# A merged attention kernel: idle mask products on TensorE at three stage starts, loads and setup work in another order, and a row sum shared with GpSimd

## The chip, the cores and the metric

The kernel runs on one core of a Trainium2 chip. The metric is the time of one execution on the device in microseconds (us), as the median of several runs. The core has TensorE (PE in the profile, with PEld for its weight loads), VectorE (DVE), ScalarE (ACT), GpSimd (POOL) and SyncE (SP), which here only issues transfers.

## The reference

Two layers are computed one after the other over 32 sequences of 112 tokens with 512 features.

```
# layer 0: gated attention to a memory of 375 rows of 256 features
mp    = memory @ W_mem
attn  = softmax(x @ mp.T / sqrt(512));  mc = attn @ mp
x     = rmsnorm(x + sigmoid([x, mc] @ W_gate.T + b) * mc) * norm_w
# layer 1: every token has one of two experts (v or l)
q,k,v = rmsnorm(x) @ (v_qkv or l_qkv), rotary on q and k
x     = x + causal_attention(q, k, v) @ (v_dense or l_dense)      # 16 heads of 32
x     = x + cross_attention(rmsnorm(x) @ cq_w, ctx @ ckv_w) @ cdense_w
x     = x + glu_mlp(rmsnorm(x), expert v or l)
```

Products are in float32 and most are split in three: high times high, high times low, low times high. ACT makes a high part, and DVE or POOL subtracts it from the source to get the low part.

## The kernel before

There are six stages, A to F, one after the other on every engine. Each engine runs its own list, in the order in which the code writes it; semaphores carry the dependencies.

**Stage A** (about 0 to 357 us in the profile) is layer 0, in 8 groups of 4 sequences. PE's list for a group is `gate(g-1)`, `attended` (probabilities times memory), `turn(g-1)`, `context(g)`, `u(g+1)` and `s0(g+1)` (scores). At the start (`g == 0`) it also has `setup_pe_wc` (a product of two weights) and `setup_pe` (small products which give each token its slot by expert). `setup_dve_slots` is a chain of some 40 tiny DVE operations that ends in a memset. DVE's list at the start is: softmax of group 0, low parts of the product of weights, `attended`, low parts of memory 1 and x 1, the setup chain, `u_low(1)`, `softmax(1)`. ACT's list begins group 0 with six chunks of weights (`ring_high`), and only then `setup_act_wc`. PE's `transposed(0, ...)` stands behind a wait for `mem_n`.

**Ring.** Weights of all stages pass through a ring of 8 chunks of 128x512: SP loads one, ACT makes its high part (L199), POOL its low part (L177), PE uses it. SP issues all transfers in one list.

**Stage B** (366 to 647) makes q, k and v for 8 tiles of up to 512 tokens; tile 0 has 256. For each tile ACT squares, DVE adds an epsilon (L929), POOL takes the power (`power`, L826), DVE scales (`norm`, L934), PE transposes (`turn`, L897). POOL has the low parts of 8 chunks ahead of `power(0)`.

**Stage C** (649 to 900) is the causal attention, one sequence a step. PE writes a mask product (L1099: a 112x112 identity by a 112x448 mask, bf16) and adds the scores (L1104); DVE takes the row maximum (L1161) and subtracts it (L1166); ACT takes the exponential (L1069); PE transposes, ACT copies out (L1063), PE multiplies by v, ACT copies (`raw`, L1066); DVE sums the 1792 probabilities of a row into 16 heads (L1172), takes the reciprocal and scales (L1181); POOL scatters the result. PE's list for step s is `scores(s)`, transposes and context of s-1, `turn_in(s + 2)` (L1088), `turn_out(s - 1)`. In 14 of the steps (3 to 8 and 10 to 17) ACT also casts 512 columns of weights. SP's list is: q and k rows of sequences 0 and 1, v of 0 to 2, then `e_weights`, `q_weights` and 8 ring chunks for stage D, and only then the q and k rows of sequence 2.

**Stages D, E, F** are the dense layer with the cross queries (907 to 1062), the cross attention one sequence a step (1064 to 1662), and the mlp. D begins with `turn_context(0)` (L1295), which waits for rows that the last scatter of C has written. E's list on PE has two steps more than sequences, in which it drains.

## Time and profile before

| | |
|---|---|
| median of 3 runs | 2385.78 us (2385.53 to 2386.26) |
| the profiled execution | 2383.2 us, span 2381.4 us |
| granted TensorE clock, mean | 0.97 |
| PE / DVE / ACT / POOL busy | 2174.7 / 1342.4 / 1073.9 / 841.8 us |
| busy share of PE | 91% |

The span is what the instructions cover; some 2 us lie around it. A granted clock of 1.00 is 2.4 GHz, one of 0.50 is 1.2 GHz. A busy share close to 100% on PE says only that products follow each other there.

### The profile page before, as it was taken

What the parts mean: (1) busy time and instruction counts of PE and PEld (TensorE: products, weight loads), DVE (VectorE), ACT (ScalarE), POOL (GpSimd) and SP (SyncE); (2) the same over time, 40 slices, a digit from 0 to 9 for tenths busy, and PEclk for the clock granted to TensorE, in tenths of its full rate; (3) what the DMA queues carried; (4) which work ended last, traced back from release to release, by engine and by line L of the source; (5) the groups of instructions that cost most, each with busy time, mean ns of one, the idle gap of its engine ahead of it and who ended that gap; (6) DMA issues with size and microseconds to landing.
All of it is one profiled execution on the core that took longest, in us unless ns stands there. A gap on an engine that the chain in (4) does not pass through costs nothing.

```text
span 2381.4 us, 46501 instructions
## 1 busy us (share of the span) xinstructions
PE 2174.7 (91%) x19368; PEld 1820.1 (76%) x19368; DVE 1342.4 (56%) x1887; ACT 1073.9 (45%) x1842; POOL 841.8 (35%) x706
## 2 busy tenths in 40 slices
PE   5899996999879988988999999997899999999998
PEld 4899985887756667876777777775788888888887
DVE  4655545877669994435666666663444434435332
ACT  4334434333157774533555555554434434334432
POOL 1101017677513213540222111110555555555553
PEclk8999998999979998997999999999899999999999
DMA  6334335565454445632111111110643443443331
GB/s 201 133 115 141 123 88 180 202 234 208 146 169 130 138 121 215 253 149 74 49 41 41 49 39 49 41 33 29 222 146 124 137 131 120 148 133 109 111 116 45
DMA packets 107057, 293.56 MB, mean 123 GB/s; under 512 B 14424, under 2 KB 18360, under 8 KB 100216
## 3 DMA queue, kind: packets, MB, share of 16 engines
q1 hardware_dynamic: 86624, 229.63, 29.9%
q0 software_dynamic: 18720, 60.29, 6.9%
q8 instruction: 154, 2.52, 0.4%
q10 hardware_dynamic: 1504, 0.68, 0.1%
q14 instruction: 55, 0.45, 0.1%
HBM read 221.36 MB, written 69.18 MB: 122 GB/s over the span
## 4 chain that ended last, share of the span: by engine, by line
PE 73%; DVE 17%; ACT 4%; DMA 3%; issue 2%; POOL 1%; SPq 0%; POOLq 0%; DVEq 0%; ACTq 0%
PE ps L109 19%; PE ps L111 18%; PE ps L110 18%; PE ps L1554 4%; PE ps L1573 3%; PE ps L1591 3%; DVE f_arena L1166 3%; DVE c_max L1161 3%; DVE f_arena L962 3%; ACT f_arena L1474 3%; DVE c_sum L1172 2%; DMA f_arena<-mem_t 1%; PE ps L607 1%; DVE f_arena L958 1%; PE ps L1576 1%
## 5 line engine op out<-in xcount | busy, mean ns | idle before, releaser
L109 PE MATMUL ps<-r_arena 128*128 128x512 f32 (+6 forms) x2410 | 905.6, 376 | 39.1 <-DVE r_arena L177 18.2
L177 POOL TENSOR_TENSOR r_arena<-f_arena,r_arena 128x512 fp32r<-128x512 f32 (+1 forms) x438 | 586.5, 1364 | 868.7 <-ACT r_arena L1455 438.4
L111 PE MATMUL ps<-r_arena 128*128 128x512 f32 (+6 forms) x2410 | 883.8, 367 | 0.0
L110 PE MATMUL ps<-r_arena 128*128 128x512 f32 (+6 forms) x2410 | 883.6, 367 | 0.0
L109 PEld LDWEIGHTS ps<-r_arena 128*128 128x128 f32 (+2 forms) x2410 | 456.0, 189 | 131.8 <-issue 37.6
L111 PEld LDWEIGHTS ps<-r_arena 128*128 128x128 f32 (+2 forms) x2410 | 455.9, 189 | 66.1
L110 PEld LDWEIGHTS ps<-r_arena 128*128 128x128 f32 (+2 forms) x2410 | 457.0, 190 | 60.1
L199 ACT CAST r_arena<-f_arena 128x512 fp32r<-128x512 f32 x400 | 235.5, 620 | 171.3 <-PE ps L111 131.7
L1675 DVE TENSOR_REDUCE e_negmax<-ps 112x3 f32<-112x1125 f32 (+1 forms) x160 | 225.2, 1408 | 106.7 <-PE ps L1554 103.8
L1474 ACT ACTIVATE f_arena<-ps 125x1792 f32<-125x1792 f32 x96 | 159.9, 1666 | 97.9 <-PE ps L1576 97.4
L1959 DVE SCALAR_TENSOR_TENSOR f_arena<-f_arena,ps 128x512 f32<-128x512 f32 (+1 forms) x88 | 57.4, 652 | 234.8 <-ACT f_arena L1850 234.8
L1854 ACT CAST r_arena<-f_arena 128x512 fp32r<-128x512 f32 (+1 forms) x88 | 52.2, 593 | 248.7 <-DVE f_arena L1963 248.7
L177 DVE TENSOR_TENSOR r_arena<-f_arena,r_arena 128x512 fp32r<-128x512 f32 (+4 forms) x141 | 111.1, 806 | 73.3 <-ACT r_arena L1854 58.0
L1573 PE MATMUL ps<-r_arena 32*125 32x224 f32 x2304 | 100.9, 285 | 39.8 <-ACT f_arena L1474 39.4
L1573 PEld LDWEIGHTS ps<-r_arena 32*125 32x125 f32 x2304 | 82.1, 185 | 66.3 <-ACT f_arena L1474 50.5
L1554 PE MATMUL ps<-r_arena 32*112 32x376 f32 x1536 | 121.4, 355 | 9.5 <-DVE e_negmax L1675 4.9
L1963 DVE SCALAR_TENSOR_TENSOR f_arena<-f_arena,ps 128x512 f32<-128x512 f32 (+1 forms) x88 | 57.6, 654 | 104.5 <-PE ps L111 104.1
L1850 ACT ACTIVATE f_arena<-ps 128x512 f32<-128x512 f32 (+1 forms) x88 | 50.2, 570 | 138.4 <-PE ps L111 138.4
L177 DVE TENSOR_TENSOR r_arena<-ps,r_arena 128x224 fp32r<-128x224 f32 (+3 forms) x130 | 75.0, 591 | 64.7 <-ACT r_arena L1257 25.1
L1034 POOL DMA_INDIRECT ctx_rows<-f_arena,slot_all x32 | 30.0, 936 | 200.2 <-DVE f_arena L1181 200.2
L1554 PEld LDWEIGHTS ps<-r_arena 32*112 32x112 f32 x1536 | 73.3, 172 | 32.9 <-DVE e_negmax L1675 14.5
L452 POOL TENSOR_TENSOR a_rstd<-a_ss,minus_half 112x2 f32<-112x2 f32 x16 | 11.3, 707 | 233.7 <-DVE a_ss L719 233.7
(197 smaller groups left out, 2714.9 us busy)
## 6 DMA issues: line engine op xcount, KB each, us to landing
f_arena<-weights SPq DMA_DIRECT2D x400, 256.0 KB, 3.0
f_arena<-rows SPq DMA_DIRECT2D x14, 1160.0 KB, 5.2
f_arena<-qk_rows SPq DMA_DIRECT2D x32, 448.0 KB, 3.9
f_arena<-mem_e SPq DMA_DIRECT2D x32, 376.0 KB, 3.1
f_arena<-mem_t SPq DMA_DIRECT2D x16, 750.0 KB, 9.8
f_arena<-mem_n SPq DMA_DIRECT2D x8, 1500.0 KB
h_rows<-f_arena SPq DMA_DIRECT2D x7, 1160.0 KB, 4.8
f_arena<-h_rows SPq DMA_DIRECT2D x7, 1160.0 KB, 5.2
```

What stands on the lines that cost most here:

```text
L109: first = pe.matmul(out, w_hi, x_hi, start=start, stop=False)
L110: pe.matmul(out, w_hi, x_lo, start=False, stop=False)
L111: return first, pe.matmul(out, w_lo, x_hi, start=False, stop=stop)
L177: return engine.tensor_tensor(out, source, high.bitcast(F32), ALU.subtract)
L199: act.copy(w_hi[:, m % RING, :], w_raw[:, m % RING, :]).then_inc(w_hi_made, 1)
L962: dve.tensor_tensor(b_qk[:, j, which * DIM:(which + 1) * DIM].rearrange("p (h d) -> p h d", h=HEADS), by_cos, by_sin, ALU.add).then_inc(b_ ...
L1161: dve.tensor_reduce(c_max[:].rearrange("p (m j) -> p m j", j=4), now, AX_X, ALU.max).then_inc(*d_steps.up())
L1166: dve.tensor_tensor(c_prob[b % 2].rearrange("p (m j) s -> p m j s", j=4), now, c_max[:].rearrange("p (m j) -> p m j", j=4).unsqueeze(3).to ...
L1474: act.activation(e_pt[:, u], ps[0:KC, 4:8, 0:4 * SEQ], ACT.Exp).then_inc(e_exp, 1)
L1554: last = pe.matmul(ps[0:SEQ, h - s_heads[u][0], 0:CEVEN], q[r, h // 4, :], k[r, h // 8, :], start=n == 0, stop=n == 2)
L1573: pe.matmul(ps[0:KC, 4 + i, out], k[r, t, m], q[r, 2 * t:2 * t + 2, :], start=n == 0, stop=False)
L1675: dve.tensor_reduce(e_negmax[:, b % 2, heads[0]:heads[-1] + 1], ps[0:SEQ, 0:len(heads), 0:CTX], AX_X, ALU.max, negate=True).then_inc(e_max ...
```

## The change

It adds idle mask products on PE (their result is never read) ahead of stages B, C and D: 64, 12 and 28 of them. It also reorders SP's, ACT's, PE's and DVE's lists at the start of A; puts POOL's `power(0)` between the fourth and the fifth low part in B; moves the loads of `e_weights`, `q_weights` and D's chunks behind those of the q and k rows of sequences 2 and 3 in C; lets POOL fold half of the heads (adds the two halves of 56 columns) so that DVE sums 896 and 448 elements in place of 1792; and writes E's last two steps out in another order.

```diff
+        def keep_busy(pe, bank, count):
+            for _ in range(count):
+                pe.matmul(ps[0:SEQ, bank, 0:NT], ident_b[0:SEQ, 0:SEQ], causal[:].rearrange("p m s -> p (m s)"),
+                          start=True, stop=True)
@@ stage A, SP @@
-            for c in range(CT, A_CHUNKS):
+            for c in range(C_MC, C_GATE):
                 ring_load(sp, c, weights[c])
+            load_memory_t(1, 0)
             load_x(1)
+            for c in range(C_GATE, A_CHUNKS):
+                ring_load(sp, c, weights[c])
+            load_memory_t(1, 1)
@@ stage A, ACT @@
                 if g == 0:
-                    for m in range(CT, RING):
+                    setup_act_wc(act)
+                    for m in range(C_MC, C_GATE):
                         ring_high(act, m)
-                    setup_act_wc(act)
-                    setup_act_consts(act)
...
                 if g == 0:
-                    memory_high(1, 1)
+                    memory_high(1, 0)
+                    setup_act_consts(act)
+                    for m in range(C_GATE, RING):
+                        ring_high(act, m)
@@ behind the four mc copies @@
+                if g == 0:
+                    memory_high(1, 1)
@@ stage A, PE @@
-                    pe.wait_ge(a_mn_loaded, 16 * (g + 1))
                     if g == 0:
                         transposed(g, 0)
                         transposed(g, 1)
+                    pe.wait_ge(a_mn_loaded, 16 * (g + 1))
...
-                if g == 0:
-                    setup_pe(pe)
                 if g + 1 < GROUPS:
                     u(g + 1)
                     s0(g + 1)
+                if g == 0:
+                    setup_pe(pe)
@@ stage A, DVE @@
-                    memory_low(1, 1)
+                    memory_low(1, 0)
                     x_low(1)
-                    setup_dve(dve)
-                    setup_dve_total(dve)
-                    setup_dve_ranks(dve)
-                    setup_dve_slots(dve)
+                    memory_low(1, 1)
                 if g + 1 < GROUPS:
                     u_low(g + 1)
+                    if g == 0:
+                        setup_dve(dve)
+                        setup_dve_total(dve)
+                        setup_dve_ranks(dve)
+                        setup_dve_slots(dve)
                     softmax(g + 1)
@@ stage B, POOL and PE @@
-            for c in range(RING):
+            for c in range(RING // 2):
                 ring_low(pool, b_chunk(0, c))
             power(0)
+            for c in range(RING // 2, RING):
+                ring_low(pool, b_chunk(0, c))
             power(1)
...
+            keep_busy(pe, 2, 64)
             turn(0)
@@ stage C, SP @@
-            sp.dma_start(e_w_raw, e_weights).then_inc(e_w_loaded, 16)
-            sp.dma_start(q_w_raw, q_weights).then_inc(e_w_loaded, 16)
-            for n in range(CT):
-                base = sp.value_load(base_d[0:1, n:n + 1], min_val=W_D, max_val=W_D + D_CHUNKS)
-                for c in range(D_CHUNKS):
-                    ring_load(sp, M_D + D_CHUNKS * n + c, chunk_at(base, c))
             for b in range(2, BATCHES):
                 sp.wait_ge(c_tk, b - 1)
                 load_qk(b)
                 if b >= 3:
+                    if b == 3:
+                        ... (the same two loads and 8 ring loads)
                     sp.wait_ge(c_ctx, b - 2)
                     load_v(b)
@@ stage C, POOL, DVE, PE @@
+            def fold(b):
+                pool.wait_ge(c_exp, b + 1)
+                if b == 0:
+                    pool.wait_ge(b_v_scattered, 16 * BLOCKS)
+                if b:
+                    pool.wait_ge(c_summed, 2 * b)
+                half = c_prob[b % 2][:, HEADS // 2:HEADS, :]
+                pool.tensor_tensor(c_fold, half[:, :, 0:SEQ // 2], half[:, :, SEQ // 2:SEQ], ALU.add).then_inc(c_folded.sem, 1)
...
-                dve.tensor_reduce(c_sum[:], c_prob[b % 2], AX_X, ALU.add).then_inc(c_summed, 1)
-                dve.wait_ge(c_summed, b + 1)
+                dve.tensor_reduce(c_sum[:, 0:HEADS // 2], c_prob[b % 2][:, 0:HEADS // 2, :], AX_X, ALU.add).then_inc(c_summed, 1)
+                dve.wait_ge(*c_folded.at(b + 1))
+                dve.tensor_reduce(c_sum[:, HEADS // 2:HEADS], c_fold, AX_X, ALU.add).then_inc(c_summed, 1)
+                dve.wait_ge(c_summed, 2 * (b + 1))
...
             pe.wait_ge(b_v, BLOCKS)
+            keep_busy(pe, 7, 12)
             turn_in(0)
@@ stage D, PE @@
+            keep_busy(pe, 0, 28)
             turn_context(0)
@@ stage E, PE, behind the loop over s < BATCHES @@
+            b = BATCHES - 1
+            maximum_turn(b)
+            scores_by_key(b, 0)
+            context(b - 1, 1)
+            turn(b - 1)
+            scores_by_key(b, 1)
+            back(b - 1)
+            scores_by_key(b, 2)
...
```

Under `if b == 3:` stand the two loads and the 8 ring loads that were taken out above. In E, PE's list goes on with `dense(30)`, both parts of `context(31)`, `turn(31)`, `back(31)` and `dense(31)`. In E, ACT's order at step 32 becomes: exponential 0, `raw`, exponential 1, copy of the turned context, `e_out` (L1507), exponential 2. Before, PE had `context(30, 1)`, `turn(30)` and `back(30)` ahead of `scores_by_key(31, 0)`.

## Rows read from the trace of the kernel before

**Rows 1.** Windows view, start of stage C: length, busy, granted clock, DMA share, GB/s

```profile
655.00:677.00 22.00, 8.22 (x58) 5.99 (x56) 4.05 (x2) 4.53 (x7) 0.00 (x0) 0.50 0.77 253
```

**Rows 2.** Timeline, stage A: start us, us, engine line op, idle before and releaser

```profile
36.95 1.57 PE L597 MATMUL ps<-ident,f_arena 112*125 112x112 f32 x6 [7.75 <-issue]
43.62 2.90 PE L607 MATMUL ps<-f_arena 125*128 125x112 f32 x12 [5.11 <-DVE f_arena L709]
58.29 0.41 PE L288 MATMUL ps<-f_arena 112*32 112x128 f32 x2 [0.28 <-DVE f_arena L315]
71.20 0.17 DVE L385 TENSOR_SCALAR f_arena<-f_arena 128x2 int32<-128x2 f32 x1
72.04 0.62 PE L109 MATMUL ps<-r_arena 128*112 128x376 f32 x1 [4.67 <-DVE r_arena L666]
76.41 1.05 DVE L673 TENSOR_REDUCE a_max<-ps 112x1 f32<-112x375 f32 x2 [3.98 <-PE ps L111]
77.75 0.36 PE L109 MATMUL ps<-r_arena 128*128 128x448 f32 x1
81.59 0.64 ACT L504 ACTIVATE f_arena<-ps,half_b 128x448 f32<-128x448 f32 x1 [1.12 <-PE ps L111]
```

**Rows 3.** Timeline, start of stage B

```profile
363.58 9.80 POOL L177 TENSOR_TENSOR r_arena<-f_arena,r_arena 128x512 fp32r<-128x512 f32 x8
370.99 2.42 DVE L929 TENSOR_SCALAR t_ss<-t_ss 128x2 f32<-128x2 f32 x1 [10.45 <-ACT f_arena L858]
374.23 0.88 DVE L934 TENSOR_SCALAR f_arena<-f_arena,t_rstd 128x512 f32<-128x512 f32 x2 [0.83 <-POOL t_rstd L826]
375.17 1.97 PE L897 MATMUL ps<-ident,f_arena 128*128 128x128 f32 x8 [18.23 <-DVE f_arena L934]
401.09 4.76 DVE L934 TENSOR_SCALAR f_arena<-f_arena,t_rstd 128x512 f32<-128x512 f32 x4 [0.90 <-POOL t_rstd L826]
```

**Rows 4.** Timeline, start of stage C

```profile
653.62 1.73 PE L1088 MATMUL ps<-ident,f_arena 112*128 112x112 f32 x8 [6.47 <-DMA f_arena<-qk_rows]
657.58 1.70 PE L1099 MATMUL ps<-causal,ident_b 112*112 112x448 bf16 x4
659.55 5.37 SPq L186 DMA_DIRECT2D f_arena<-weights  x8
664.97 0.91 SPq L1006 DMA_DIRECT2D f_arena<-qk_rows  x2
674.12 1.76 PE L1088 MATMUL ps<-ident,f_arena 112*128 112x112 f32 x8 [13.06 <-DMA f_arena<-qk_rows]
679.22 2.02 DVE L1161 TENSOR_REDUCE c_max<-ps 112x16 f32<-112x1792 f32 x1 [14.01 <-PE ps L1104]
```

**Rows 5.** Groups of DVE in 677 to 900: count, busy us, mean ns, idle before

```profile
L1172 DVE TENSOR_REDUCE c_sum<-f_arena 112x16 f32<-112x1792 f32 x32 | 64.3, 2008 | 0.0
```

**Rows 6.** Timeline, steady steps of stage C

```profile
683.06 0.53 ACT L1066 COPY f_arena<-ps 128x448 f32<-128x448 f32 x1 [0.52 <-PE ps L1126]
684.18 0.92 PE L1099 MATMUL ps<-causal,ident_b 112*112 112x448 bf16 x4
686.16 2.02 DVE L1161 TENSOR_REDUCE c_max<-ps 112x16 f32<-112x1792 f32 x1
689.78 0.53 ACT L1066 COPY f_arena<-ps 128x448 f32<-128x448 f32 x1 [0.52 <-PE ps L1126]
745.69 1.70 ACT L1069 ACTIVATE f_arena<-f_arena 112x1792 f32<-112x1792 f32 x1
752.63 1.70 ACT L1069 ACTIVATE f_arena<-f_arena 112x1792 f32<-112x1792 f32 x1
```

**Rows 7.** Timeline, start of stage D

```profile
906.83 1.97 PE L1295 MATMUL ps<-ident,f_arena 128*128 128x128 f32 x8 [7.62 <-DMA f_arena<-ctx_rows]
```

**Rows 8.** Chain that ended last, start of stage D

```profile
912.97 1.75 PE ps L1295 x16
```

**Rows 9.** Timeline, end of stage E

```profile
1655.71 1.36 PE L1591 MATMUL ps<-f_arena 125*32 125x112 f32 x48 [0.48 <-ACT f_arena L1474]
```

More of the change, by code:

```diff
@@ L414, in a_sp, with load_memory_t @@
         def a_sp(sp):
-            def load_memory_t(g):
-                for t in range(CT):
-                    sp.wait_ge(a_m_lo, CT * g + t)
-                    sp.dma_start(memt, mem_t[g][:, t, :]).then_inc(a_mt_loaded, 16)
+            def load_memory_t(g, t):
+                sp.wait_ge(a_m_lo, CT * g + t)
+                sp.dma_start(memt, mem_t[g][:, t, :]).then_inc(a_mt_loaded, 16)
             def load_x(g):
@@ L434, in a_sp @@
             load_memory_n(0)
-            for c in range(CT, A_CHUNKS):
+            for c in range(C_MC, C_GATE):
                 ring_load(sp, c, weights[c])
+            load_memory_t(1, 0)
             load_x(1)
+            for c in range(C_GATE, A_CHUNKS):
+                ring_load(sp, c, weights[c])
+            load_memory_t(1, 1)
             for g in range(1, GROUPS):
-                load_memory_t(g)
                 if g >= 2:
+                    for t in range(CT):
+                        load_memory_t(g, t)
                     sp.wait_ge(a_fused, KT * (g - 1))
@@ L505, in a_act @@
                                        bias=half_b[:, t:t + 1], scale=0.5).then_inc(a_tanh, 1)
-                    if t in ((0, 3) if g else (0,)) and g + 1 < GROUPS:
+                    if g and t in (0, 3) and g + 1 < GROUPS:
                         memory_high(g + 1, t // 3)
@@ L754, in a_dve @@
                     attended(0, 1)
-                    memory_low(1, 0)
                 if g < GROUPS:
@@ L991, in build_xattn @@
             "c_pt", "c_pt_made", "c_ctx", "c_raw", "c_turned", "c_out", "c_summed"))
+        c_folded = Later(a_powered, 2 * GROUPS)
         c_scattered = [sem(f"c_scattered{i}") for i in range(2)]
@@ L1027, in c_sp @@
                 if b >= 3:
+                    if b == 3:
+                        sp.dma_start(e_w_raw, e_weights).then_inc(e_w_loaded, 16)
+                        sp.dma_start(q_w_raw, q_weights).then_inc(e_w_loaded, 16)
+                        for n in range(CT):
+                            base = sp.value_load(base_d[0:1, n:n + 1], min_val=W_D, max_val=W_D + D_CHUNKS)
+                            for c in range(D_CHUNKS):
+                                ring_load(sp, M_D + D_CHUNKS * n + c, chunk_at(base, c))
                     sp.wait_ge(c_ctx, b - 2)
@@ L1507, in e_act @@
                     act.copy(e_out[b % 2], ps[0:SEQ, 3, :]).then_inc(e_cd_out, 1)
+                if 1 <= s < BATCHES:
+                    exponents(s - 1, 1)
                 if 1 <= s <= BATCHES:
-                    for u in range(1, KEY_UNITS):
-                        exponents(s - 1, u)
+                    exponents(s - 1, 2)
         def e_pe(pe):
@@ L1627, in e_pe @@
             scores(0, 0)
-            for s in range(BATCHES + 2):
+            for s in range(BATCHES):
                 if s < 2:
@@ L1633, in e_pe @@
                     keys(s + 1)
-                if 1 <= s <= BATCHES:
+                if s:
                     maximum_turn(s - 1)
-                if s < BATCHES:
-                    scores(s, 1)
+                scores(s, 1)
                 if s >= 2:
@@ L1647, in e_pe @@
                     back(s - 2)
-                if s < BATCHES:
-                    scores(s, 2)
-                if 1 <= s <= BATCHES:
+                scores(s, 2)
+                if s:
                     scores_by_key(s - 1, 0)
@@ L1653, in e_pe @@
                     dense(s - 2, 0)
-                if s < BATCHES:
-                    scores(s, 3)
+                scores(s, 3)
                 if s >= 2:
                     dense(s - 2, 1)
-                if 1 <= s <= BATCHES:
+                if s:
                     scores_by_key(s - 1, 1)
-                if s < BATCHES:
-                    scores(s, 4)
-                if 1 <= s <= BATCHES:
+                scores(s, 4)
+                if s:
                     scores_by_key(s - 1, 2)
@@ L1665, in e_pe @@
                     scores(s + 1, 0)
-                if 1 <= s <= BATCHES:
+                if s:
                     context(s - 1, 0)
+            b = BATCHES - 1
[6 more added lines that the diff above has]
+            scores_by_key(b, 2)
+            for k in range(CT):
+                dense(b - 1, k)
+            for t in range(CT):
+                context(b, t)
+            turn(b)
+            back(b)
+            for k in range(CT):
+                dense(b, k)
         def e_dve(dve):
```

13 lines of the change are left out of this document (10 added, 3 removed).

## The prediction, as it was put on record

> **What bounds the kernel now.** The page first. PE is busy for 91% of the span and the mean granted clock is 0.97, so in A, B, D, E and F the sum of the products is nearly the time; idle mask products cannot shorten these. What can be had lies where PE stands still or runs at 1.2 GHz, and in C, where it is not the bound. So I read the windows view at the borders of the stages and found four holes, then the timeline of each.
>
> (a) Start of C. In 22 us PE is busy for 8.2 and the clock is 0.50 [rows 1]. The timeline says why: SP issues the q and k rows of sequence 2 at 665.0, behind 8 ring chunks and two larger loads, and PE gets them at 674.1 [rows 4]. PE's list has `turn_in(2)` ahead of `scores(1)`, so DVE waits 14.0 us for its second maximum [rows 4].
>
> (b) Steps of C. DVE's maximum comes back after 6.94 us [rows 4, 6]; DVE has no idle time in them, and one of its four larger operations is the row sum of 2.01 us [rows 5]. But two other loops are close behind. ACT's exponential comes back after 6.94 us in a step with a cast [rows 6], with nothing idle between. And in the step from 683.06 to 689.78, which has no cast and in which ACT's copy (L1066) sets PE's start, that copy comes back after 6.72 us: turn out, masks, scores, transposes, four copies, context, copy [rows 6]. The reader is to see three loops: DVE 6.94, ACT and PE 6.72, ACT with a cast 6.94.
>
> (c) Start of A: PE has the memory rows at 36.95 but starts `attended` only at 43.62, because DVE stands in its list behind the low parts of the weight product [rows 2]. Later `s0(1)` waits 4.7 us for `u_low(1)`, which stands behind the setup chain on DVE [rows 2].
>
> (d) Starts of B and D: PE idles 18.2 and 7.6 us for data and starts at half clock [rows 3, 7].
>
> **The sum, part by part.**
>
> *Stage C, order of the loads.* The bytes between v and the q/k rows of sequence 2 are 1 MB, 0.5 MB and 8 times 0.25 MB. Without them those rows are issued some 7 us earlier, at about 658, with only 0.7 MB of v ahead. I take 661.5 for their landing. DVE's first maximum and subtraction end at 665.2 (679.22 less the 14.01 idle) [rows 4]; `scores(1)` cannot begin before that. At half clock masks and scores take some 3.6 us (four masks are 1.70) [rows 4], so the second maximum would be at 668.8 and the gain 10.4. What is queued behind the moved loads: v of 3 and q/k of 4 wait for SP to issue the ten loads (about 6 us), and are needed two steps later; ACT waits for `e_weights` at step 2, over 10 us after their issue. I cost both at nothing; if cover failed, each would cost its lateness once, under 3 us.
>
> *Stage C, 12 masks.* They follow 2.4 us after the last product of B (PE's idle time began at 647.15 [rows 4]) and end before the first rows come at 653.62, at either pace: at full clock 12 are at most 2.8 (four in 0.92, so at most 0.23 each), at half at most 5.1 (four in 1.70, so at most 0.43) [rows 4, 6]; the latter would end at 654.4, 0.8 late. If the clock stays at 2.4 GHz, both `turn_in`, masks and scores of two steps are faster: 2.2 us by the first maximum, 1.5 by the second, together up to 3.7. But PE has gaps of one to two us there that could bring the clock down again. I take 2.1 of 3.7. Start of C together: 12.5, between 9 and 14.
>
> *Stage C, the fold.* 1792 elements take 2.01 us [rows 5]. A maximum over 375 takes 0.53 (two in 1.05 [rows 2]), so an element costs 1.48 / 1417 = 1.04 ns; by this line, an estimate, 896 and 448 take 1.07 and 0.61, and the two overlap a little: 0.37 less a step. POOL's fold of 448 is about 1.1 us (a low part of 512 is 1.22 [rows 3]), can begin with the sum of the step before and is due a whole step later; hidden. But the loop of ACT and PE allows 0.21 only (6.94 less 6.72), in the 17 steps without a cast; in the 14 with one nothing. 17 x 0.21 = 3.6. Bounds: 0, and 31 x 0.37 = 11.5.
>
> *Stage B.* `power(0)` stands behind eight low parts, to 373.4; DVE's epsilon, ready at 371.0, takes 2.42 us for two columns [rows 3]: it is held up until POOL is through. With four low parts ahead, POOL is free at 368.5, the power is made at 371.9 and `norm(0)` can begin 2.3 us earlier. But now four low parts run beside it. Where that is so, `norm` took 4.76 us for four operations [rows 3], 1.19 each, against 0.44 each alone. So two take 2.4 in place of 0.88, and 1.5 of the 2.3 are lost. If they wait for all four low parts (to 376.8), they end at 377.7, 2.6 late. The 64 masks start at 356.9; at full clock they take at most 14.7 and end by 371.6, ahead of `turn(0)`; at half clock at most 27.5, and they could hold PE up. They follow dense products without a gap, so I take the former and 0.1 for a faster `turn(0)`. Sum 0.9, between -2.5 and 2.5.
>
> The Trainium skill, "SBUF — State Buffer", section Who interferes with whom, says that a `tensor_scalar` may take the port pair that VectorE and GpSimd share, as an exclusive lock for a whole instruction, while a reduction never does. The long epsilon agrees with it. By the rule the fold disturbs none of DVE's sums in C, as I assume, and `norm(0)` is held up as I cost it. It speaks against the new place of `power(0)`: if POOL keeps the pair from one low part to the next, the case with 377.7 is the one.
>
> *Stage A.* `attended` starts at 36.95 in place of 43.62, now that DVE's lows of the weight product come before the chunks (PE then waits for memory alone). From 43.62 to 58.29 is `attended` and `context`, 14.7 with some waits; then `u(1)` of 24 products at 0.205, the wait for its lows (1.5) and `s0(1)`, 5.7 (72.04 to 77.75, cold) or 4.2 warm [rows 2]. New: 36.95 + 14.7 + 4.9 + 1.5 + 4.2 = 62.3, against 77.75. But `softmax(1)` stands behind the setup chain, and this chain now needs `setup_pe`, which is behind `s0(1)`. From `setup_pe` to the chain's end were 13.1 us (58.29 to 71.37), of which about one is done earlier now: `softmax(1)` at 74.4 against 76.41. ACT has its exponentials ahead of the `tanh` that PE's third tile of `gate(0)` waits for: 4.1 us later (81.59 less 1.12 less 76.41) they are done, tanh 0.64, so PE goes on at 79.1. Before, the third tile began at 85.4 (77.75 and two tiles of 3.8) [rows 2]. Gain 6.3, less 1.5 because PE idles some 7 us and restarts at half clock (`s0(1)` above shows the price: 5.7 for 4.2), less 1.5 for DVE's `x_low(1)` and `memory_low` beside POOL's low parts. 3.3, between 0 and 6.
>
> *Stage D, 28 masks.* They start when C's last turn ends (899.2, 906.83 less 7.62 [rows 7]), at half clock after C's thin tail. If the clock rises after some 4 us of them (10 masks), as it did behind other starts, they take 8 us: about 907, with the rows at 906.83. At 2.4 GHz the 8 transposes and the 12 products behind them, which now take 6.1 us (to 912.97 [rows 8]), take some 4. Gain 1.9; all masks at half clock (12.0) would make it -4.3, which I take as the lower end.
>
> *Stage E.* The last exponential moves behind `e_out(30)`, which waits for `dense(30)`. Walking the new order with the rows' durations puts it at 1655.9 against 1655.7 [rows 9]. Nothing, within 1 either way.
>
> Sum: 12.5 + 3.6 + 0.9 + 3.3 + 1.9 + 0 = 22.2. The profiled execution of 2383.2 (its span and 1.8 around it) becomes 2361.0; it lies 2.6 under the median, so the median becomes 2363.6.
>
> **Rivals.**
> 1. *The fold pays in full.* DVE has no idle time, which speaks for it; the 6.72 of ACT and PE and the 6.94 with a cast speak against. Gain 11.5 for 3.6: 2355.7. 0.12.
> 2. *POOL keeps the port, and A's head start is spent on waits.* By the lock of the epsilon row, `norm(0)` ends 2.6 late (-3.5 against mine), and A gives 0 (-3.3): 2370.4. 0.15.
> 3. *The moved loads only move the wait.* If the rows of sequence 2 were late for another reason, such as v's scatter at the end of B, the start of C would give 4 in place of 12.5: 2372. The 3.5 MB ahead of them speak against it. 0.06.
> 4. *Slower: the fold holds DVE up.* If each fold stopped a DVE operation for its length of 1.1 us, 31 steps would grow by 1.1 less 0.2: 28 us against the other 18.6, so 2395. It decides from 0.6 us a step. POOL's stream holds the epsilon of B up, which speaks for it; that POOL runs low parts in 14 of C's steps and the mean sum is 2.01 all the same [rows 5] speaks against. 0.03.
>
> My forecast has 0.64.
>
> **From cases to numbers.** 2363.6, range 2354 to 2372: rivals 1 and 2 lie in it, 3 at its edge, 4 outside. 0.2% is 4.8 us, about what a measurement of this kernel can tell from no change. Faster by more 0.95, within 0.02, slower 0.03.
>
> **What would show it.** Second maximum of C near 666 in that profile less the shifts of A and B, with no wait for q/k rows; steps of 6.7 and 6.9, with DVE idle behind the scores; L1172 as two groups near 1.07 and 0.61; `norm(0)` near 1.2 us each; the third tile of `gate(0)` after about 7 us of idle PE; masks in B ending before the norm; stage D's first second at full clock. Wrong would be: masks that end after their data, a wait of DVE for the fold, or a new wait of C's steps 2 to 4 for rows or v.

## The result, and the profile after

The changed kernel takes 2372.64 us (median of 4 runs, 2371.06 to 2374.28) against 2386.02 (4 runs) of the kernel before beside it: a ratio of 0.9943, 95% interval 0.9926 to 0.9960. The gain is 13.4 us where 22.2 were forecast, and the time lies 0.6 us above the range. Its profiled execution is the longest of the four: 2374.28 us, span 2372.4, mean granted clock 0.975.

Three more series of the unchanged kernel, each beside the kernel before, gave 0.9920 (0.9904 to 0.9937), 0.9928 (0.9914 to 0.9941) and 0.9929 (0.9910 to 0.9949). The mean of the four ratios is 0.9930, some 16.7 us. The forecast was 0.9907. So the sign held, and the largest term, the load order, held too. A quarter of the forecast gain is missing by the mean of the four series, and 40% of it by the first.

First the windows view, columns as in [rows 1] (length; busy us of PE, PEld, DVE, ACT and POOL; granted clock; DMA share; GB/s). The first line answers to [rows 1]. It is the same stretch after the last copies of v, which come 1.8 us sooner now: PE is busy for 15.3 us of 22 and not 8.2, and the clock is 0.77 and not 0.50. The next three lines of the changed kernel are places where PE ran at half clock and where nothing had been forecast. The last line is of the kernel before, at the end of E: full clock throughout.

```profile
653.20:675.20 22.00, 15.25 (x187) 11.35 (x188) 10.74 (x9) 9.04 (x14) 2.12 (x2) 0.77 0.88 283
376.00:392.00 16.00, 13.46 (x59) 11.28 (x58) 10.66 (x21) 8.48 (x19) 8.64 (x7) 0.86 0.29 86
1044.00:1052.00 8.00, 6.62 (x43) 6.62 (x44) 1.33 (x3) 0.89 (x2) 1.61 (x2) 0.79 0.28 108
1638.00:1656.00 18.00, 12.01 (x146) 8.80 (x146) 1.47 (x4) 4.43 (x7) 1.87 (x2) 0.72 0.15 47
...
1643.00:1662.00 19.00, 12.78 (x265) 9.44 (x265) 2.77 (x7) 7.24 (x8) 0.93 (x1) 1.00 0.15 45
```

Then the timeline, start of A (answers to [rows 2]), of B ([rows 3]) and of C ([rows 4]). The lines are of the changed kernel, apart from the one at 384.15, which is `turn(1)` of B in the kernel before.

```profile
37.25 2.90 PE L620 MATMUL ps<-f_arena 125*128 125x112 f32 x12 [5.16 <-DMA f_arena<-mem_n]
80.53 0.74 PE L109 MATMUL ps<-r_arena 128*128 128x448 f32 x1 [7.79 <-ACT f_arena L512]
...
353.07 12.27 PE L216 MATMUL ps<-causal,ident_b 112*112 112x448 bf16 x64
368.83 5.30 POOL L177 TENSOR_TENSOR r_arena<-f_arena,r_arena 128x512 fp32r<-128x512 f32 x4
368.87 2.89 DVE L951 TENSOR_SCALAR f_arena<-f_arena,t_rstd 128x512 f32<-128x512 f32 x2 [0.83 <-POOL t_rstd L840]
371.82 1.97 PE L913 MATMUL ps<-ident,f_arena 128*128 128x128 f32 x8 [6.48 <-DVE f_arena L951]
380.80 3.50 PE L913 MATMUL ps<-ident,f_arena 128*128 128x128 f32 x16 [2.54 <-DVE f_arena L951]
...
384.15 1.97 PE L897 MATMUL ps<-ident,f_arena 128*128 128x128 f32 x16 [3.15 <-DVE f_arena L934]
...
647.48 2.48 PE L216 MATMUL ps<-causal,ident_b 112*112 112x448 bf16 x12 [2.14 <-ACT f_arena L901]
651.72 0.99 PE L1119 MATMUL ps<-ident,f_arena 112*128 112x112 f32 x8 [1.75 <-DMA f_arena<-qk_rows]
653.50 1.66 PE L1119 MATMUL ps<-ident,f_arena 112*128 112x112 f32 x8 [0.80 <-DMA f_arena<-qk_rows]
654.91 1.59 SPq L1028 DMA_DIRECT2D f_arena<-v_rows  x3
656.54 0.89 SPq L1025 DMA_DIRECT2D f_arena<-qk_rows  x2
657.92 2.02 DVE L1193 TENSOR_REDUCE c_max<-ps 112x16 f32<-112x1792 f32 x1 [13.85 <-PE ps L1135]
663.95 1.75 PE L1119 MATMUL ps<-ident,f_arena 112*128 112x112 f32 x8 [6.11 <-DMA f_arena<-qk_rows]
665.50 1.70 PE L1130 MATMUL ps<-causal,ident_b 112*112 112x448 bf16 x4
668.32 2.02 DVE L1193 TENSOR_REDUCE c_max<-ps 112x16 f32<-112x1792 f32 x1 [6.32 <-PE ps L1135]
```

The reader is to see: `attended` starts 6.4 us sooner, but PE stands 7.8 us ahead of the third tile of `gate(0)`; the epsilon takes 0.17 and not 2.42 (its row starts at 367.88), but `norm(0)` takes 2.89 beside POOL's low parts; the 64 masks end at 365.3, and 6.5 us later `turn(0)` runs at half clock as before; `turn(1)` takes 3.5 us for 16 transposes, where the kernel before had 1.97, behind a wait of 3.15 us. At C the second maximum is at 668.3 (679.2 in [rows 4]), and PE still waits 6.1 us for the rows of sequence 2, though they are issued 8.4 us sooner.

DVE's groups in stage C ([rows 5]) and two exponentials in a step with a cast and two in one without ([rows 6]):

```profile
L1204 DVE TENSOR_REDUCE c_sum<-f_arena 112x8 f32<-112x896 f32 x32 | 34.4, 1075 | 0.0
L1206 DVE TENSOR_REDUCE c_sum<-f_arena 112x8 f32<-112x448 f32 x32 | 19.5, 609 | 0.0
```

```profile
741.24 1.70 ACT L1100 ACTIVATE f_arena<-f_arena 112x1792 f32<-112x1792 f32 x1
748.18 1.70 ACT L1100 ACTIVATE f_arena<-f_arena 112x1792 f32<-112x1792 f32 x1
...
870.54 1.70 ACT L1100 ACTIVATE f_arena<-f_arena 112x1792 f32<-112x1792 f32 x1
872.32 1.14 POOL L1064 TENSOR_TENSOR f_arena<-f_arena 112x448 f32<-112x448 f32 x1 [4.17 <-ACT f_arena L1100]
877.21 1.70 ACT L1100 ACTIVATE f_arena<-f_arena 112x1792 f32<-112x1792 f32 x1
```

6.94 with a cast and 6.67 without; the sums take 1.08 and 0.61, as the line through the two rows had it, and DVE never waits for the fold (L1064).

Start of D ([rows 7]; the last line is of the chain of work, [rows 8]) and end of E ([rows 9]):

```profile
885.86 7.10 PE L216 MATMUL ps<-causal,ident_b 112*112 112x448 bf16 x28
893.78 1.10 PE L1329 MATMUL ps<-ident,f_arena 128*128 128x128 f32 x8 [0.82 <-DMA f_arena<-ctx_rows]
...
898.18 1.75 PE ps L1329 x16
```

```profile
1641.67 0.63 PE L111 MATMUL ps<-r_arena 128*112 128x512 f32 x1
1643.02 4.38 PE L1631 MATMUL ps<-f_arena 125*32 125x112 f32 x96 [0.72 <-issue]
1650.78 0.77 PE L109 MATMUL ps<-r_arena 128*112 128x512 f32 x1 [0.86 <-DVE r_arena L177]
1653.72 0.59 ACT L1546 COPY f_arena<-ps 112x512 f32<-112x512 f32 x1 [3.42 <-PE ps L111]
```

The masks end 0.8 us before D's rows come, and the first turn is at full clock. So it was in two more of the four profiles. In the third the masks ran at full clock all along, took 5.5 us, ended 2.3 us before the rows, and the turn ran at half clock (1.96). In E's tail, in the execution shown, most of the last two `dense` and the 96 products of the last context run at half clock: 0.63 for 512 columns, where the kernel before had 0.40, and 4.38 for 96, where it had 1.36 for 48.

**Stage by stage.** One execution is moved by a microsecond or two by the places where the clock falls. So the table takes the time between two marks in several profiles: two of the kernel before, four of the changed one. A mark is the start of a row of the timeline; a merged row, such as the four last copies of v, has the start of its first instruction.

```
us                                   before          changed (4)                   gain   forecast
start to turn(0) of B            375.17 374.91   371.82 371.55 371.55 371.56       3.4     4.2
turn(0) to last copy of v        272.01 272.02   273.56 273.67 273.94 272.22      -1.3     0
copy of v to second maximum       32.04  32.67    22.94  22.28  22.97  21.18      10.0    12.5
second to last maximum of C      207.83 207.82   204.78 204.79 204.79 204.72       3.1     3.6
last maximum to last output       12.26  12.66    13.06  12.67  12.12  13.08      -0.3     0
to the last turn_normed of D     156.72 156.30   155.02 155.24 155.98 155.05       1.2     1.9
to the first maximum_turn of E    47.02  49.10    49.00  47.01  49.06  48.97      -0.5     0
E's tail (last maximum_turn to
  last copy to e_out)             19.18  20.08    22.91  22.90  22.27  22.91      -3.1     0
from there to the end            719.25 716.35   718.68 718.69 718.73 718.91      -1.0     0
```

The gains are differences of the means. They add up to 16.1 at the end of D's products and to 11.5 over all rows. One stretch isn't in the table, the body of E: 539.9 and 539.4 before, and 540.6, 543.6, 544.8 and 537.1 after. With its 1.9 us the profiled executions differ by 9.6 us in the mean. Two of the four bodies are 4.8 us longer for a reason that is not of this change (last section), which is 2.4 in the mean; so the timed gain, not the 9.6, measures the change.

Forecast row 1 is A's 3.3 and B's 0.9; all of B's forecast gain lay there. Its 3.4 is on the high side. In eleven other profiles with the same code in A, with the masks and without, `turn(0)` of B came at 371.6 to 373.6.

### The profile page after: what moved, and what is told of

The parts are those of the page before. It is cut to its first block, busy times and chain, and to the rows that moved or that the text cites. A ratio compares the mean times of both kernels' runs of the same rounds, so it can differ in the third digit from the quotient of the medians.

```text
span 2372.4 us, 46806 instructions
## 1 busy us (share of the span) xinstructions
PE 2201.2 (93%) x19472; PEld 1838.7 (78%) x19472; DVE 1335.8 (56%) x1919; ACT 1072.9 (45%) x1842; POOL 880.1 (37%) x738
## 4 chain that ended last, share of the span: by engine, by line
PE 78%; DVE 9%; ACT 7%; DMA 3%; issue 2%; POOL 1%; SPq 0%; POOLq 0%; DVEq 0%; ACTq 0%
PE ps L109 19%; PE ps L111 18%; PE ps L110 18%; PE ps L1594 4%; PE ps L1631 4%; PE ps L1613 3%; DVE f_arena L979 3%; ACT f_arena L1509 2%; PE ps L1146 2%; ACT f_arena L1094 1%; DMA f_arena<-mem_n 1%; PE ps L620 1%; DVE f_arena L975 1%; PE ps L1157 1%; DVE f_arena L971 1%
## 5 line engine op out<-in xcount | busy, mean ns | idle before, releaser
L1594 PEld LDWEIGHTS ps<-r_arena 32*112 32x112 f32 x1536 | 73.6, 173 | 32.8 <-DVE e_negmax L1727 14.4
L979 DVE TENSOR_TENSOR f_arena<-f_arena 128x512 f32<-128x512 f32 x60 | 91.4, 1524 | 2.1
```

Of the source, the lines that this page charges most:

```text
L979: dve.tensor_tensor(b_qk[:, j, which * DIM:(which + 1) * DIM].rearrange("p (h d) -> p h d", h=HEADS), by_cos, by_sin, ALU.add).then_inc(b_ ...
L1594: last = pe.matmul(ps[0:SEQ, h - s_heads[u][0], 0:CEVEN], q[r, h // 4, :], k[r, h // 8, :], start=n == 0, stop=n == 2)
```

## The experiments

They came in four groups, each timed beside runs of the kernel before, whose medians in the groups were 2393.84, 2383.57, 2393.79 and 2385.34 us. Times are to be compared inside a group, or by ratio; the intervals reach some 3 to 5 us to either side, so the marks carry the argument.

**1. The changed kernel again** (three times, no edit).

> The changed kernel once more, nothing edited. Two theories of why 15 us gained by the start of D were only 9.0 at the end of the profiled run. (1) The losses belong to the code: this run's profile then has the same half-clock stretches (1046 to 1049, 1640 to 1647, turn(1) of B at 381) within 1 us, and a span of 2372. (2) They are chance, a matter of the moment at which a gap of PE falls: some of these stretches are gone or stand elsewhere, and the span differs by 1 to 4 us, with the difference in D and E. The timed median stays near 2372.6 in both cases.

> The changed kernel a third time, as the measure for the three kernels beside it, and for what repeats from one execution to the next. What repeats belongs to the change: turn(1) of B at half clock (3.5 us for 16), second maximum of C 22 to 23 us behind the last copy of v, steps of C of 6.7, the tail of E (from the last maximum_turn to the last e_out copy) 22.9 us against 19.2 and 20.1 in two profiles of the kernel before. What does not repeat is chance: the end of D and the start of E, 47.0 or 49.0 us.

> The changed kernel as the measure for the three beside it: from turn(0) of B to the last copy of v 273.6 to 273.9 us, turn(1) of 16 transposes 3.5 us, the tail of E 22.3 to 22.9 us.

Medians 2375.80, 2377.68 and 2367.04 us. The second profile against the first, the stretch in which D's last queries run:

```profile
1044.00:1052.00 8.00, 6.01 (x48) 5.81 (x48) 0.35 (x1) 2.14 (x4) 2.62 (x3) 1.00 0.24 94
376.00:392.00 16.00, 13.54 (x59) 11.39 (x58) 10.91 (x21) 8.42 (x18) 8.80 (x7) 0.86 0.26 80
```

Here the clock didn't fall at 1046 (0.79 in the first profile, 1.00 in this one, in the same code), but it did again at 381. Both theories hold, each for other places. What repeats is `turn(1)` of B (granted clock 0.85 or 0.86 in 376 to 392, four of four) and E's tail. D's end with E's start takes 47 or 49 us by chance, in the kernel before as well.

**2. The kernel before again.**

> The kernel before once more, nothing edited, for a second profile. If the difference that opens behind 908 us is chance (when the clock falls in a gap of PE, and how long ACT takes to start in E), this profile shows other half-clock stretches in D and E than the first, and a span that differs by 1 to 7 us; the stage marks up to the last maximum of C stay within 1 us of the first (second maximum 679, last one 887). If it is the code, both profiles of the kernel before agree within 0.5 us throughout.

Span 2381.3, the first 2381.4; but 49.1 in place of 47.0 at the start of E, and 2.9 us less from E's last output to the end. Up to the end of C both agree within 1 us.

**3. Loads held back until the q/k rows have landed.**

```diff
                     if b == 3:
+                        sp.wait_ge(c_qk_loaded[0], 32)
+                        sp.wait_ge(c_qk_loaded[1], 32)
                         sp.dma_start(e_w_raw, e_weights).then_inc(e_w_loaded, 16)
```

> The changed kernel, but SP waits until the q and k rows of sequences 2 and 3 have landed before it issues e_weights, q_weights and the 8 chunks. Theory: the rows of sequence 2 took 7.4 us from issue to landing because these loads shared the DMA engines with them; alone they land in some 3.5 us, PE's second turn_in group starts at about 660 instead of 664, the second maximum comes at about 664.5 instead of 668.3, and the kernel gains 3.5 us (2369). Rival: the rows are slow for another reason (the v rows ahead of them, their own size); then they land after 7 us as before and nothing is gained (within 0.5 us). A second rival: the loads are now late for ACT's first cast, a wait there of some 2 us, which would eat half of the gain.

```profile
657.60 0.90 SPq L1025 DMA_DIRECT2D f_arena<-qk_rows  x2
663.19 1.76 PE L1121 MATMUL ps<-ident,f_arena 112*128 112x112 f32 x8 [3.67 <-DMA f_arena<-qk_rows]
```

With nothing behind them the rows take 5.6 us, not 3.5. In the first three profiles of the changed kernel PE had them at 664.0, 662.5 and 663.9, 7.4 us after issue in the first; in the fourth, with all ten loads behind them as ever, at 660.4, 4.2 us after issue (656.14). So what follows the rows doesn't decide alone. What goes ahead may, which these rows suggest and don't show: the q/k rows of sequence 4 are issued here just behind the 8 chunks, and PE had them at 679.53, 7.8 us from issue. With that wait and a stretch at half clock behind it the steps of C took 3.2 us more (207.95). 2378.66 us against 2375.80: the theory falls.

```profile
671.75 0.43 SPq L1025 DMA_DIRECT2D f_arena<-qk_rows  x1
679.53 0.98 PE L1121 MATMUL ps<-ident,f_arena 112*128 112x112 f32 x8 [1.50 <-DMA f_arena<-qk_rows]
```

**4. The q/k rows of sequence 2 ahead of v.**

```diff
+            sp.wait_ge(c_tk, 1)
+            load_qk(2)
             sp.wait_ge(b_v_scattered, 16 * BLOCKS)
             for b in range(3):
                 load_v(b)
-            for b in range(2, BATCHES):
+            for b in range(3, BATCHES):
```

> The changed kernel, but SP issues the q and k rows of sequence 2 as soon as turn_in(0) has freed their buffer, ahead of the wait for v's scatter and the three v loads. New theory of why these rows came at 664: with e_weights, q_weights and the chunks held back they still landed 5.6 us after issue, so most of the lateness lies in their issue at 656.5, behind v's scatter (654.8) and 0.7 MB of v. Here they are issued at about 653 and land by 658; scores(1) then waits for DVE's subtraction (about 662) and not for rows, the second maximum comes at 665.5 instead of 668, and 2 to 3 us are gained. Rival: v of sequence 0 now comes so late that context(0) waits, and nothing is gained.

```profile
659.14 1.48 PE L1121 MATMUL ps<-ident,f_arena 112*128 112x112 f32 x8
663.51 1.63 PE L1132 MATMUL ps<-causal,ident_b 112*112 112x448 bf16 x4 [2.89 <-DVE f_arena L1200]
666.98 2.02 DVE L1195 TENSOR_REDUCE c_max<-ps 112x16 f32<-112x1792 f32 x1 [3.62 <-PE ps L1137]
```

PE no longer waits for rows but for DVE's subtraction (L1200): the wait that the forecast had named as the floor. The second maximum comes 7.7 us after the first (10.4, 8.3, 10.5 and 7.1 in the changed kernel) and 21.6 after the copy of v, 0.7 less than the changed kernel's mean. Ratio 0.9940 (0.9923 to 0.9956), in another group: no gain that the time can show. The lateness is where the new theory has it, and the edit takes the wait away; what it was worth is 0.7 in the mean, not 2 to 3, as the fourth profile of the changed kernel had its rows early by itself.

**5. Without masks, masks alone, without the fold.**

> The changed kernel without the 64, 12 and 28 mask products. By my sum the masks gave 0.1 in B, 2.1 at the start of C and 1.9 at the start of D, so it would be 4 us slower. By what the changed kernel's trace shows it is less: in B turn(0) ran at half clock with the masks as well, and turn(1) took 3.5 us with them and 2.0 in the kernel before; without masks turn(1) is at full clock again and B gains 1.5. At C both turn_in groups take 1.7 again (1.0 and 1.7 with masks), at D the eight transposes 2.0 (1.1 with masks). Together 1 to 2.5 us slower. Rival: the clock's later course changes with them so that nothing is left of it, within 0.5 us.

> The kernel before with the 64, 12 and 28 masks alone. The run without masks says that they do little: the start of C took 22.7 us without them and 22.3 to 23.2 with them, and the eight transposes that open B ran at half clock either way. So: B and C unchanged within 0.5 us, D 1.1 us less if the eight transposes of its first turn and the products behind them run at 2.4 GHz, the whole 0.5 to 1.5 us faster than before, which its time cannot show and its stage marks can. Rival: with PE's rows of sequence 0 two us later than in the changed kernel the masks end too early and the clock is half again at C (4 masks 1.70).

> The changed kernel without the fold: DVE sums all 1792 elements again, POOL does nothing in their place. Theory (three loops): steps of 6.94 us again, from the second maximum to the last 3.1 to 3.6 us longer, the time 3.3 us more. Rival (the fold pays in full, 0.37 in each of 31 steps): 11.5 us more. Rival (the fold holds DVE up through the shared port): the changed kernel's steps would be as long, and this one is not slower.

Without masks: ratio 0.9945 (0.9928 to 0.9962). C's start takes 22.7 us (22.3 in the mean with them), D up to its last turn 156.15 (155.3 with them), B 273.7. So the load order is worth 9.6 us (32.36 in the mean of the kernel before, less 22.73). For the 12 masks 0.4 is left, less than the four profiles with them differ among themselves (21.2 to 23.0), and for the 28 masks 0.8. It reaches `turn(0)` 1.6 us later, but that was lost in A, ahead of the first mask. Its `turn(1)` fell to half clock too:

```profile
373.26 1.97 PE L913 MATMUL ps<-ident,f_arena 128*128 128x128 f32 x8 [18.52 <-DVE f_arena L950]
382.24 2.98 PE L913 MATMUL ps<-ident,f_arena 128*128 128x128 f32 x16 [3.63 <-DVE f_arena L950]
```

The masks of B thus neither warmed `turn(0)` (1.97 with and without) nor are they what cools `turn(1)`. Masks alone on the kernel before: 2391.77 us against 2393.79, ratio 0.9991 (0.9981 to 1.0001). C's start 32.8, as without them; D 155.1. By this ratio some 2 of 17 us, and at the most 4.5, come from the idle products that the title names first. The run without masks would leave them 3.6 (0.9945 against the mean of 0.9930), inside the intervals.

Without the fold the steps from the second to the last maximum took 208.0 us, 3.2 more than the 204.8 with it, and the sums are back in one group:

```profile
L1202 DVE TENSOR_REDUCE c_sum<-f_arena 112x16 f32<-112x1792 f32 x32 | 64.3, 2008 | 0.0
```

So the fold gives what the three loops allow. Neither rival holds: not 11.5 us, and no loss.

**6. POOL's old order at the start of B.**

```diff
-            for c in range(RING // 2):
+            for c in range(RING):
                 ring_low(pool, b_chunk(0, c))
             power(0)
-            for c in range(RING // 2, RING):
-                ring_low(pool, b_chunk(0, c))
```

> The changed kernel with POOL's eight low parts ahead of power(0) again; the masks and everything else stay. Theory (port): the earlier power gains little, because norm(0) then takes 2.9 us beside POOL's low parts and not 0.9; here power(0) comes some 2 us later, norm(0) takes 0.9, turn(0) starts within 0.5 us of 371.8, and the time is within 0.7 us of the changed kernel's. Rival: the earlier power is worth its whole 2.3 us; then this kernel is 2 us slower. Beside that the second turn may fall at half or at full clock, which would show as 1.5 us either way at 381.

`norm(0)` takes 0.88 there and `turn(0)` starts at 372.00 (371.82). But equal code had `turn(0)` anywhere from 371.6 to 373.6. From the last transposes of A to `turn(0)` it is 20.7 us here, and 20.5 to 21.0 in the four profiles of the changed kernel. So the earlier power is worth 0.2 us or nothing, not 0.8. The median, 2376.21 against 2375.80, says the same.

**7. Twelve masks ahead of `turn(1)`.**

```diff
+                    if c == 2 and n == 0:
+                        keep_busy(pe, 2, 12)
                     if c == 2 and n + 1 < TILES:
                         turn(n + 1)
```

> The changed kernel with 12 idle mask products ahead of turn(1) of stage B, where PE waits 2.5 us. If the clock falls in this wait, they keep it at 2.4 GHz: turn(1) takes 2.0 in place of 3.5, the step from turn(1) to turn(2) 21.8 in place of 23.4, and B is 1.5 us shorter. Rival: the fall was set in motion earlier, by the idle 6.5 us ahead of turn(0) and the thin products behind it; then turn(1) stays at half clock, and the masks give nothing.

```profile
379.65 2.43 PE L216 MATMUL ps<-causal,ident_b 112*112 112x448 bf16 x12
382.15 1.97 PE L913 MATMUL ps<-ident,f_arena 128*128 128x128 f32 x16
```

`turn(1)` takes 1.97 again, from it to the next turn 21.78 (23.3 to 23.4 in the changed kernel, 21.8 before). The 1.5 us are the clock, and PE's wait of 2.5 us just ahead is the place where masks pay. The time, 2369.45 against 2367.04, can't show 1.5 us.

**8. E's tail.** The old order twice, and the new one with 24 masks in its waits (`keep_busy(pe, 0, n)` with n 2, 4, 6, 3, 3, 3 and 3 ahead of the steps for which PE waits).

> The changed kernel with the end of stage E in the order of the kernel before, on PE and ACT. In the profiled run the last e_out copy had 12.2 us of gain before the tail and 8.4 behind it. (1) If the new order costs time by itself, this kernel is some 2 to 3.7 us faster (about 2369.5). (2) If it was only that the clock fell at 1640 in the new order, in about every run, the same gain, and the profile shows the old order at full clock until the last dense. (3) If both orders are equal and the clock falls in either now and then, the change is within 1 us.

> The changed kernel with the old order of E's tail, a second time. If the new order costs 3 us by itself, the tail takes 19.2 to 20.1 here, as in the kernel before, and the time is 3 us less than the changed kernel's. If the clock decides whatever the order, the tail takes 22.3 again, with a half-clock stretch in it, and the time is the same within 1 us.

> The changed kernel with idle mask products in the gaps of E's new tail (24 in all, two to six in each wait of PE). If the tail is long because the clock falls in it (PE stands still for about 1 us four times, and its dense(30) and the 96 products of the last context then run at half clock), the masks hold the clock, and the tail takes 19 to 20 us in place of 22.9: 3 us gained. If the order itself is the longer one, or the clock falls all the same, nothing is gained or some tenths lost.

The old order took 22.3 and 19.2 us, the new one with masks 19.4. The timeline, first the old order's second profile, then the new order with masks:

```profile
1641.59 1.36 PE L1626 MATMUL ps<-f_arena 125*32 125x112 f32 x48 [0.48 <-ACT f_arena L1509]
1646.33 0.49 PE L109 MATMUL ps<-r_arena 128*112 128x512 f32 x1 [0.86 <-DVE r_arena L177]
```

```profile
1646.58 1.36 PE L1631 MATMUL ps<-f_arena 125*32 125x112 f32 x48 [0.16 <-ACT f_arena L1509]
1651.31 0.49 PE L109 MATMUL ps<-r_arena 128*112 128x512 f32 x1 [0.29 <-DVE r_arena L177]
```

At full clock the two orders are equal, as forecast (`best3`, below, has 19.2 with the new one). The new one took 22.05 to 22.91 in all eleven profiles that had it without masks, with part of it at half clock; the old one 19.2, 19.2, 20.1, 22.3 and 22.3 in five. Both 22.3 are of the groups in which the body of E was 4.8 us longer (last section). In the other groups the old order had 19.2 to 20.1 three times of three, and the new one 22.9 six times of six. So the order and the execution decide together whether the clock falls. `e_tail_masks` has the ratio 0.9917 against 0.9928 beside it (2372.33 and 2377.68 us); the old order 2375.03 against 2375.80 and 2368.82 against 2367.04, no difference that can be told.

**9. More holes filled, and all together.** `filled_gaps` is the changed kernel with edit 4, 96 masks in place of 64, and 12, 20 and 48 masks ahead of D's last queries, E's first keys and F's first turn. `best3` adds edit 7 and the masks of 8.

> A further kernel: the changed one with the q and k rows of sequence 2 issued ahead of v, 96 masks in place of 64 ahead of B (so that they end at 371.5, just before turn(0)), and masks in three more holes: 12 ahead of the last cross queries of D (PE stands 2.5 us), 20 ahead of the first keys of E (5 us) and 48 ahead of the first turn of F (11 us). Theory: a half-clock stretch follows each such hole and costs half of PE's busy time in it. B gains 1.0 at turn(0) and perhaps 1.5 at turn(1), C 0.7 to 1.7, D's end 0 to 1.5, E's start 1.5, F's start 2 to 2.9: 6 to 9 us less than the changed kernel. Rival: the clock falls a little later instead, as it did in C and E, and only C's part stays, 1 us.

> All that helped, together: the changed kernel with the q and k rows of sequence 2 ahead of v, masks in E's tail, 96 masks ahead of B, 12 ahead of turn(1), and masks at the end of D and the starts of E and F. If the parts add up (6.2 of filled_gaps, 3.5 of E's tail, 1.5 at turn(1) if that holds) it is 8 to 11 us faster than the changed kernel; if the clock only falls somewhere else instead, 5 to 6.

`filled_gaps`: 2371.46 us against 2377.68 of the changed kernel beside it, 0.9912 (0.9897 to 0.9927). D's end and E's start took 45.7 (47 or 49), B 272.1. C's start took 21.9. The 96 masks ended 0.5 us before `turn(0)`, and here it ran at full clock, 1.10 us for 1.97: what the 64 lacked was length. The next turn came 0.4 us sooner for it. `turn(1)` took 3.3 all the same. F gained nothing: its turn ran at full clock behind the 48 masks, and the clock fell right after. The first line is `turn(0)`, the others are F.

```profile
371.57 1.10 PE L913 MATMUL ps<-ident,f_arena 128*128 128x128 f32 x8 [0.49 <-DVE f_arena L951]
...
1650.07 9.36 PE L216 MATMUL ps<-causal,ident_b 112*112 112x448 bf16 x48
1661.42 1.09 PE L1925 MATMUL ps<-ident,f_arena 128*128 128x128 f32 x8 [1.98 <-DVE f_arena L1987]
1664.94 0.41 PE L109 MATMUL ps<-r_arena 128*128 128x256 f32 x1
```

`best3` is the fastest of all: 2361.49 us against 2367.04 of the changed kernel and 2385.34 of the kernel before, ratio 0.9904 (0.9889 to 0.9918); its profiled execution has span 2353.4 and a mean clock of 0.989. The last 34 us up to F's turn, all at full clock:

```profile
1616.00:1650.00 34.00, 29.69 (x423) 21.00 (x424) 5.89 (x15) 10.80 (x15) 2.59 (x3) 1.00 0.32 114
```

It is 5.5 us faster than the changed kernel by the medians, at the lower of the two expectations, and the intervals of the two overlap; by the spans of the profiled executions it is 12.3, but there its fastest of four executions (2355.27 to 2365.23) stands against a middle one. In that execution the clock didn't fall in F either, and from E's last output to the end took 715.4 us, 3.3 less than in the changed kernel; `filled_gaps` had the same masks there and 718.3.

## Why the prediction was right and wrong

The forecast missed its range because three terms of its sum were wrong: E's tail, put at nothing, lost 3.1 us; the masks of C, put at 2.1, gave 0.4; and B, put at a gain of 0.9, lost more at `turn(1)` than it won. One step failed in all three: products behind short waits of PE were priced, wholly or in part, at full clock, and they ran at half.

**Right: the load order, in kind.** Three and a half megabytes in front of the q/k rows were what held C up. It gave 9.6 of the 10.4 forecast. The landing, put at 661.5 in the old profile (659.7 in the new one), came at 662.5 to 664.0 in three profiles of four: "with only 0.7 MB of v ahead" was read as a small thing, but v itself isn't issued until its scatter has ended (654.9), the rows come behind it, and they took 4.2 to 7.4 us (experiments 3 and 4). The 8.4 us that they are issued sooner were forecast as 7.

**Wrong: the 12 masks, 2.1 of 3.7.** They ended where I said, and in three profiles of the four the first `turn_in` was at full clock (0.99); in the fourth the clock fell in the masks themselves (1.76). In the first profile the clock fell behind it: the two next `turn_in` took 1.66 and 1.75, and the masks of both steps 1.70. The fear in the text, gaps of one to two us, was the case and deserved the larger weight. And what the first maximum won by it was lost in waiting for rows. Measured 0.4, within the spread. (At half clock the 12 would have ended at 654.7 by the terms given, not at 654.4; nothing hung on it.)

**Wrong: B, 0.9 forecast.** Three parts. The port: `norm(0)` took 2.89 for the forecast 2.4, which leaves 0.3 of the 0.8, and experiment 6 finds 0.2 at the most. The masks: I took 14.7 us for 64, "at most", and so had them end some 3 us before `turn(0)`; at 0.19 each they took 12.3, ended 6.5 us early, and `turn(0)` ran at half clock. With 96, which ended 0.5 us before it, it did not (experiment 9). The clock at `turn(1)`, which nothing in the forecast priced, cost 1.5 (experiment 7). Why it fell there in every profile of the changed kernel, also without masks and with the masks alone, and in neither of the kernel before, where PE waits as long, was not settled. The length of the wait alone doesn't decide it: 3.15 us in the kernel before, 2.3 to 2.5 in the changed one.

The Trainium skill, "SBUF — State Buffer", section Who interferes with whom, gives VectorE and GpSimd one port pair with an exclusive lock. The rows agree in kind: 2.89 us beside POOL's low parts, 0.88 without. Its stricter reading, in which `norm(0)` would have waited for all four (rival 2), was not the case: the two norms ran between them.

**Wrong: E's tail, 0 forecast, 3.1 lost.** Walking the new order with the rows' durations was right at full clock (19.4 with masks, 19.2 for the old order). The step that failed is that I took those durations as given: with the new order the clock fell somewhere in the tail in each of the eleven profiles without masks, and with masks in its waits (`e_tail_masks`, `best3`) it didn't, but for the first microsecond of one of the two. Which wait does it is not shown. The old order has waits of the same length (0.65 to 1.76 us), and the stretch at half clock lay on both last contexts in some executions and ahead of them and behind them in others.

**Nearly right.** A: `attended` from 37.25 (36.95 forecast), the third tile of `gate(0)` at 80.5 (79.1), PE idle for 7.8 (7); the end of `gate(0)` 3.0 sooner (3.3). A was not taken apart by a run. The fold: 3.1 to 3.2 of 3.6, steps of 6.67 to 6.72 and of 6.94 as written (7.00 where the casts begin). D: 1.2 of 1.9, 0.8 of it by the masks; they took 7.1 to 7.7 us in three profiles (8 forecast) and 5.5 in the other.

**The rivals.** Rival 1 is refuted by `no_fold` (3.2, not 11.5), rival 4 too. Rival 3 named a true wait, v's scatter, but it costs 1 to 3 us, not 8. Rival 2's time, 2370.4, is near the measured one for other reasons: half of its mechanism (the port) is there for 0.6 us, and A gave its 3. By the marks the rows of the table fall short of the forecast by 2.5 at C's start, 2.1 in A and B, 3.1 in E's tail, 0.7 in D and 0.5 in C's steps; the other 1.7 lie in rows for which nothing was forecast, and there the two profiles of the kernel before differ by as much or more.

## What to carry to other kernels

Let idle products end within a microsecond of the work that they are to warm. In these profiles the first turn or `turn_in` behind a block of 12 or more was at full clock in all ten cases with a gap of up to 1.2 us (apart from two in which the clock fell in the products themselves), in 14 of 24 with a gap of 1.7 to 2.8 us, and in none of 13 with 5.9 to 6.9. What they win is soon lost again if further waits follow in which the clock can fall; fill the last wait, not the longest one. Count them by their own duration at full clock, not by a bound. When an order is rewritten by hand with durations from a profile at full clock, ask for each short wait that it makes whether the clock will stay; and when a transfer is late, move its issue first, ahead of what waits for another engine, before looking for contention behind it.

## What the runs showed that was not expected

The same code met the clock's fall in some executions and not in others: D's last queries ran at 0.79 or 1.00 in the changed kernel, and D's end with E's start took 47 or 49 us in both kernels. A difference of 2 us between two single profiles says nothing here.

Eight steps of E, those in which ACT also casts a chunk for F, took 17.5 us each in some profiles and 18.1 in all eight of two of the groups of runs, in the same code: 4.8 us in all. In those groups the kernel before took 2393.8 us, in the others 2383.6 to 2386.0. ACT stands idle for 1.83 us ahead of its third exponential there, and for 1.24 otherwise; why, no run shows. The 4.8 us are half of the 10 by which the groups differ.

One tile of B (from `turn(3)` to `turn(4)`) took 34.4, 36.0 to 36.3 or 37.2 to 37.3 us with the same instructions. DVE was busy in it for 26.3 to 27.3 us in the shortest cases and for 28.2 to 30.3 in the others; that its rotary products ran more or less beside POOL's low parts is a guess.
